# A transformer stack with its residual stream kept centred: layer norms that skip the mean, and variances and their spread in column and row groups

## The reference

```python
def _layernorm(x, axis=-1, eps=1e-05):
    m = jnp.mean(x, axis=axis, keepdims=True)
    v = jnp.var(x, axis=axis, keepdims=True)
    return (x - m) / jnp.sqrt(v + eps)

x = x + windowed_attention(_layernorm(x))      # stage 0, 16 heads of 8, output weights Wo
x = x + ffn(_layernorm(x))                     # stage 1, ternary weights, bias
x = x + gated_recurrence(_layernorm(x))        # stage 2, ends in gelu(..) @ ld_W + ld_b + identity
x = x + ffn(_layernorm(x))                     # stage 3, the same weights as stage 1
x = x + full_attention(_layernorm(x)) + bo     # stage 4, Wo of layer 1
x = x + moe(_layernorm(x))                     # stage 5, top-1 router over 8 experts, one shared We
x = x + full_attention(_layernorm(x))          # stage 6, W_out
x = x + moe(_layernorm(x))                     # stage 7, the same weights as stage 5
```

## Time and profile before

| | us |
|---|---|
| median of three runs | 1211.13 |
| the profiled execution, device time | 1204.97 |
| its span in the profile | 1203.2 |
| PE busy | 1051.9 (87%) |
| DVE busy | 864.4 (72%) |
| ACT busy | 748.8 (62%) |
| POOL busy | 90.4 (8%) |

### The profile page before, as it was taken

The page is one execution under the profiler, slowest core; times in us unless marked ns, Lnnn a source line. Parts: engine busy times, 40 slices in busy tenths (PEclk is TensorE's granted clock), DMA queues, the critical chain, the costliest instruction groups (busy, mean ns, idle before and its releaser), DMA issues.

```text
span 1203.2 us, 31909 instructions
## 1 busy us (share of the span) xinstructions
PE 1051.9 (87%) x13025; PEld 484.6 (40%) x13025; DVE 864.4 (72%) x1151; ACT 748.8 (62%) x1510; POOL 90.4 (8%) x370
## 2 busy tenths in 40 slices
PE   7598999794587999899999998779898899999986
PEld 3344545442253333334444344442333334344443
DVE  3553654345554799899999944555999999999635
ACT  2422545237213389889999982231888899999921
POOL 8000100000000000000000000000000000000000
PEclk9897999888778999999999997789999999999978
DMA  3473432100006322220101000044313201001000
GB/s 96 138 211 72 98 92 74 39 1 1 0 0 189 86 64 63 55 51 18 29 19 24 24 20 10 1 124 140 71 44 72 53 18 25 22 18 30 18 15 35
DMA packets 73825, 64.97 MB, mean 54 GB/s; under 512 B 27792, under 2 KB 53648, under 8 KB 73552
## 3 DMA queue, kind: packets, MB, share of 16 engines
q1 hardware_dynamic: 73680, 62.94, 20.0%
HBM read 27.06 MB, written 35.85 MB: 52 GB/s over the span
## 4 chain that ended last, share of the span: by engine, by line
DVE 43%; PE 38%; DMA 7%; issue 4%; ACT 4%; SPq 3%; DVEq 0%; ACTq 0%
DVE nmf L1331 35%; PE wide L556 24%; PE bank L556 14%; DMA KQs<-m_dram 4%; ACT xcsq L949 2%; DVE xcsq L1148 1%; DVE res L1148 1%; SPq L378 1%; DVE nmt L1290 1%; ACT big L949 1%; SPq L309 1%; DVE big L1410 1%; SPq L299 1%; DVE x L1148 1%; DMA qf_dram<-big 1%
## 5 line engine op out<-in xcount | busy, mean ns | idle before, releaser
L1331 DVE TENSOR_REDUCE nmf<-wide 128x1 f32<-128x1024 f32 x512 | 587.3, 1204 | 40.4 <-PE wide L556 40.3
L949 ACT ACTIVATE big<-wide 128x512 f32<-128x512 f32 (+1 forms) x703 | 403.4, 601 | 81.1 <-PE wide L556 54.7
L556 PE MATMUL wide<-big,KQs 48*128 48x512 bf16 (+1 forms) x1376 | 349.4, 344 | 4.3 <-DVE nmf L1331 3.3
L556 PE MATMUL bank<-big,V 128*9 128x128 f32 x8192 | 319.9, 274 | 12.5
L556 PE MATMUL wide<-KQs,big 50*128 50x512 bf16 (+1 forms) x1035 | 266.9, 324 | 11.9 <-DMA KQs<-m_dram 10.8
L556 PEld LDWEIGHTS bank<-big,V 128*9 128x9 f32 x8192 | 176.8, 90 | 233.7 <-ACT big L949 221.7
L949 ACT ACTIVATE big<-bank 128x512 f32<-128x512 f32 (+2 forms) x473 | 233.8, 516 | 23.2 <-PE bank L556 10.6
L556 PE MATMUL bank<-KQs,big 50*128 50x512 bf16 x341 | 130.3, 382 | 6.8 <-DMA KQs<-m_dram 6.8
L556 PEld LDWEIGHTS wide<-KQs,big 50*128 50x128 bf16 x1035 | 70.6, 95 | 117.9 <-ACT big L949 56.5
L1296 DVE TENSOR_REDUCE nmw<-wide 95x4 f32<-95x512 f32 (+1 forms) x96 | 61.2, 640 | 58.9 <-PE wide L556 57.9
L949 ACT ACTIVATE xcsq<-xcsq 128x512 f32<-128x512 f32 x32 | 20.1, 630 | 124.2 <-DVE xcsq L1148 124.2
(11 more groups left out here) (175 smaller groups left out, 833.3 us busy)
## 6 DMA issues: line engine op xcount, KB each, us to landing
o_dram<-big SPq DMA_DIRECT2D x128, 64.0 KB
big<-kf_dram SPq DMA_DIRECT2D x32, 200.0 KB
kf_dram<-big SPq DMA_DIRECT2D x24, 256.0 KB, 4.2
qf_dram<-big SPq DMA_DIRECT2D x24, 256.0 KB, 4.0
KQs<-qf_dram SPq DMA_DIRECT2D x32, 192.0 KB
ow_dram<-scr SPq DMA_DIRECT2D x32, 142.5 KB
big<-kw_dram SPq DMA_DIRECT2D x16, 275.0 KB
kw_dram<-scr SPq DMA_DIRECT2D x12, 352.0 KB, 5.7
```

Source lines behind the costliest of these rows:

```text
L556: return nc.tensor.matmul(o, l, r, start=start, stop=stop, **kw)
L949: return nc.scalar.activation(o, i, f, **kw)
L1331: nc.vector.tensor_reduce(nmf[:, (s0 + i) % 4, c:c + 1], wide[:, k:k + 2, :].rearrange("p g c -> p (g c)"), AX.X, ALU.max, negate=True).th ...
```

## The change

1. **Weights and biases centred.** After the ternary matrix is built in stage 0, DVE takes from each of five output weight matrices (`wo0`, `ld`, `wo1`, `wo2`, the ternary one) its mean over output channels, kept in `wmean`, and from three bias columns their channel mean, summed in `bmean`. So stages 0 to 4 and 6 add nothing to the channel mean of `x`.
2. **Means in a side tile.** `track` multiplies `wmean`'s column, broadcast to 32 columns, with the input of each output projection: four matmuls of 128 columns, each into its own group of 32 partitions of bank 0. ACT copies that bank in the next norm (`keep_means`), and POOL adds it to `mrow` (`add_means`).
3. **Layer norm.** Means are computed only in stages 0 and 6 (`MEANS`), where `x` is centred in place. In the others ACT squares `x` itself. The variance of a chunk comes from four matmuls with 32 columns of `meanw` as weights, each into its group of 32 partitions; root and reciprocal work on 128 x 128; and the spread is four matmuls over 32 partitions each, with a selector `rowsel` as weights, into four banks (0 to 3). The diagonal is gone. `normalise` reads the four banks.
4. **Work called inside the norm.** In stages 1, 3, 5 and 7 the first `ffn` or `logits` step of a chunk stands between PE's third and fourth spread, the other three behind the fourth.
5. **Mixture of experts.** Two of the `we` matmuls move behind `tri` and `ones`; ACT evacuates the `we` products with their bias instead of the gates. In stage 7 the tracked mean and `bmean` are added back to `x` by `true_x`, four DVE operations in two pairs, after 16 matmuls that spread `mrow`.
6. `keep_busy` in stage 0 also waits for `b_sum`, and POOL's first constants are joined by `rowsel` (five memsets).

```diff
@@ constants, POOL
             step(pool.memset(meanw[:, :], 1.0 / P))
+            step(pool.memset(rowsel[:, :], 0.0))
+            for g in range(4):
+                step(pool.memset(rowsel[32 * g:32 * g + 1, :], 1.0))
...
+            def add_means(t):
+                pool.wait_ge(mt_evac, t + 1)
+                pool.tensor_tensor(mrow[:, :], mrow[:, :], mtmp[:, :], ALU.add).then_inc(mt_add, 1)
@@ PE
+            def track(c, i, chunk):
+                for g in range(4):
+                    ins = mm(bk(TRACK)[32 * g:32 * g + 32, P * c:P * c + P], wmean[:, i:i + 1].broadcast_to((P, 32)),
+                             chunk[:, P * g:P * g + P])
+                if c == NC - 1:
+                    ins.then_inc(mt_mm, 1)
...
                 def variance(c):
                     pe.wait_ge(ln_sq, NC * k + c + 1)
-                    if c:
-                        pe.wait_ge(ln_std, NC * k + c)
-                    for t in range(4 * c, 4 * c + 4):
-                        ins = mm(bk(3)[:, t:t + 1], sq[:, P * t:P * t + P], meanw[:, 0:1])
+                    if c >= 2:
+                        pe.wait_ge(ln_std, NC * k + c - 1)
+                    for g in range(4):
+                        ins = mm(bk(4 + c % 2)[32 * g:32 * g + 32, 0:P], meanw[:, 0:32], xch(sq, c)[:, P * g:P * g + P])
                     ins.then_inc(ln_var, 1)
 
                 def spread(c):
-                    pe.wait_ge(ln_diag, NC * k + c + 1)
-                    if c == 2:
-                        pe.wait_ge(xn_ready, NC * k + 1)
-                    mm(bk(LN_STD[c]), ones[:, :], res[:, c % 2, :]).then_inc(ln_b, 1)
+                    pe.wait_ge(ln_rstd, NC * k + c + 1)
+                    if c == 0:
+                        pe.wait_ge(mt_evac, tracked + 1)
+                    else:
+                        pe.wait_ge(xn_ready, NC * k + c)
+                    for g in range(4):
+                        ins = mm(bk(g)[:, P * c:P * c + P], rowsel[32 * g:32 * g + 32, :],
+                                 ln_rstd_s[32 * g:32 * g + 32, P * c:P * c + P])
+                    ins.then_inc(ln_b, 1)
...
-                for step, c in ((mean, 0), (mean, 1), (variance, 0), (mean, 2), (variance, 1), (spread, 0),
-                                (mean, 3), (variance, 2), (spread, 1), (variance, 3), (spread, 2), (spread, 3)):
-                    step(c)
+                if k in MEANS:
+                    for step, c in ((mean, 0), (mean, 1), (variance, 0), (mean, 2), (variance, 1), (mean, 3)):
+                        step(c)
+                else:
+                    variance(0)
+                    variance(1)
+                spread(0)
+                variance(2)
+                spread(1)
+                variance(3)
+                spread(2)
+                if after:
+                    after(0)
+                spread(3)
+                if after:
+                    for c in range(1, NC):
+                        after(c)
...
+                mm(bk(6)[:, 8:11], meanw[:, :], bias[:, BI["ld_b"]:BI["ld_b"] + 3]).then_inc(b_mean, 1)
                 mm(bk(6)[:, 0:1], ones[:, :], ts_[:, 0:1]).then_inc(tw_sum, 1)
...
                 pe.wait_ge(tw, 2)
+                pe.wait_ge(b_sum, 1)
                 keep_busy(2, bk(6))
...
                     pe.wait_ge(at_out, NC * layer + c + 1)
+                    track(c, 1 + layer, xch(aT, c))
                     mm(bk(4 + c), w("wo%d" % layer), xch(aT, c)).then_inc(o_mm, 1)
...
+                mm(bk(4 + c), tern[:, :], xn(c)).then_inc(f_mm, 1)
+                if c == NC - 1:
+                    for j in range(NC):
+                        track(j, 4, xn(j))
+            def logits(k, c):
+                pe.wait_ge(xn_ready, NC * (5 + 2 * k) + c + 1)
+                for t in range(4 * c, 4 * c + 4):
+                    ins = mm(bk(4)[:, t * E:(t + 1) * E], xnt(t), wgs[:, :])
...
             def moe(k):
...
+                if k:
+                    pe.wait_ge(mt_add, 7)
+                    for c in range(NC):
+                        for g in range(4):
+                            ins = mm(bk(g)[:, P * c:P * c + P], rowsel[32 * g:32 * g + 32, :],
+                                     mrow[32 * g:32 * g + 32, P * c:P * c + P])
+                    ins.then_inc(mt_spread, 1)
+                expert(0)
+                expert(1)
                 pe.wait_ge(moe_const, 1)
                 pe.wait_ge(m_dve, M_DVE * k + 10)
-                mm(bk(1)[:, 0:P], tri[:, :], moh[:, :]).then_inc(m_pe, 1)
-                mm(bk(2)[:, 0:P], ones[:, :], moh[:, :]).then_inc(m_pe, 1)
+                mm(bk(6)[:, 0:P], tri[:, :], moh[:, :]).then_inc(m_pe, 1)
+                mm(bk(6)[:, P:2 * P], ones[:, :], moh[:, :]).then_inc(m_pe, 1)
+                if k:
+                    pe.wait_ge(x_out, NC)
+                expert(2)
+                expert(3)
@@ ACT
+                def keep_means():
+                    act.wait_ge(mt_mm, tracked + 1)
+                    if tracked >= 2:
+                        act.wait_ge(mt_add, tracked - 1)
+                    fn(mtmp[:, :] if tracked else mrow[:, :], bk(TRACK), ACT.Copy).then_inc(mt_evac, 1)
+
+                square(0)
+                square(1)
...
+                else:
+                    keep_means()
+                    root(0)
+                    square(2)
+                    root(1)
+                    square(3)
+                root(2)
+                root(3)
@@ DVE
                 def rstd(c):
                     dve.wait_ge(ln_std, NC * k + c + 1)
-                    r = ln_s[:, 1, 4 * c:4 * c + 4]
-                    nc.vector.reciprocal(r, ln_s[:, 0, 4 * c:4 * c + 4]).then_inc(ln_rstd, 1)
...
-                    spread(c % 2, r).then_inc(ln_diag, 1)
+                    nc.vector.reciprocal(ln_rstd_s[:, P * c:P * c + P], ln_std_s[:, P * c:P * c + P]).then_inc(ln_rstd, 1)
 
                 def normalise(c):
                     dve.wait_ge(ln_b, NC * k + c + 1)
-                    tt(xn(c), xch(xc, c), bk(LN_STD[c]), ALU.mult).then_inc(xn_ready, 1)
...
+                    tt(quarters(xn(c)), quarters(xch(x, c)), wide[:, 0:4, P * c:P * c + P], ALU.mult).then_inc(xn_ready, 1)
+
+                if k in MEANS:
+                    for c in range(NC):
+                        centre(c)
+                for step, c in ((rstd, 0), (rstd, 1), (normalise, 0), (rstd, 2), (normalise, 1), (rstd, 3),
+                                (normalise, 2), (normalise, 3)):
                     step(c)
...
+                def true_x(c):
+                    if c == 0:
+                        dve.wait_ge(mt_spread, 1)
+                        dve.wait_ge(b_sum, 1)
+                    v = quarters(xch(x, c))
+                    nc.vector.scalar_tensor_tensor(v, wide[:, 0:4, P * c:P * c + P], bmean[:, 0:1], v, ALU.add,
+                                                   ALU.add).then_inc(x_out, 1)
...
                     ternary()
+                    centre_biases()
+                    centre_weights()
                     zero_heads()
```

More of the change, by code:

```diff
@@ L543, in _ @@
                     split_shift(u, nmw[0:QT, u % 4, :], QT)
+            for t in range(1, min(nst, 4)):
+                add_means(t)
             for layer in (1, 2):
                 if nst > 2 * layer + 2:
+                    add_means(2 * layer + 2)
                     for i in range(SLOTS):
@@ L934, in _ @@
                 if stage in (1, 3):
-                    ffn(stage // 2)
+                    layernorm(stage, stage, lambda c: ffn(stage // 2, c))
                 if stage == 2:
@@ L1125, in moe @@
                 for c in range(NC):
-                    act.wait_ge(m_pe, M_PE * k + 7 + c + 1)
-                    fn(xch(mgb, c), bk(c), ACT.Copy).then_inc(m_act, 1)
+                    act.wait_ge(m_pe, M_PE * k + (2 + c if c < 2 else 4 + c))
+                    fn(xch(mgb, c), bk(WE[c]), ACT.Identity, bias=bcol("be")).then_inc(m_act, 1)
             act.wait_ge(ln_const, 1)
             for stage in range(nst):
-                layernorm(stage)
+                layernorm(stage, stage)
                 if stage == 0:
@@ L1173, in layernorm @@
-                for step, c in ((centre, 0), (centre, 1), (centre, 2), (rstd, 0), (centre, 3), (rstd, 1),
-                                (normalise, 0), (rstd, 2), (normalise, 1), (rstd, 3), (normalise, 2), (normalise, 3)):
-                    step(c)
+                    tt(quarters(xn(c)), quarters(xch(x, c)), wide[:, 0:4, P * c:P * c + P], ALU.mult).then_inc(xn_ready, 1)
+                if k in MEANS:
+                    for c in range(NC):
+                        centre(c)
+                for step, c in ((rstd, 0), (rstd, 1), (normalise, 0), (rstd, 2), (normalise, 1), (rstd, 3),
+                                (normalise, 2), (normalise, 3)):
+                    step(c)
@@ L1177, in ternary, with centre_biases @@
+            def centre_biases():
+                dve.wait_ge(b_mean, 1)
+                m = bk(6)[:, 8:11]
```

(8 more changed lines are left out.)

124 lines of the change are left out of this document (84 added, 40 removed).

## The result

The changed kernel took 1177.65 us in the median of four runs (1174.44 to 1179.17); the kernel before took 1213.99 us beside it (four runs, 1206.11 to 1218.67). The ratio is 0.970, with a 95% interval of 0.964 to 0.976: faster by 36 us, where 39 were forecast. The profiled execution after is the slowest of its four (1179.17 us, span 1177.2 us); the one before (1204.97 us, span 1203.2 us) is faster than all four beside the change. So the two traces differ by only 26.0 us, and what follows accounts for these 26.

What follows compares the result with a forecast made beforehand. Attentions hold most of the chain but stay; the gain lies in norms, chains of hand-overs between engines. Terms -41 - 8 + 0.8 + 4.5 - 5.9 + 8.3 + 2 = -39.3 us give 1172 us, range 1153 to 1192.

Steps and rivals of the forecast that it cites:

- The norms: Six norms without means: 49.9 us against 90.8, so -41 us, bounds -46 and -36.
- R: In six norms without means, end of the first root counted from the last addition to `x`: 4.65 us in sum.
- Rival 1: Float32 row pieces of spreads do not overlap: 1186 us at full clock (chance 0.13), about 1212 at half (0.05).
- Rival 3: Changes of tiling drain PE, about 60 on the path: at 0.85 us more each 1223 us, slower; chance 0.04.
- the first matmuls at 1.2 GHz: Behind norms, two to four matmuls opening recurrence and both projections cost 0.86 us more each: +4.5 us (0, +8).
- Rival 2: PE stays at 1.2 GHz in all short stages, everything at its upper bound: -20 us, 1191 us; chance 0.06.
- Tracks: Tracks ahead of output projections in stages 0, 4 and 6, three times four, mostly at 1.2 GHz: +8.3 us (+5, +9).
- `b_sum`: In stage 0 the `keep_busy` block starts later, waiting for the bias operations: +2 us (+1.7, +2.3), all on the chain.
- `centre_weights`: In stage 0 it delays `zero_heads` by 3.4 us, within the `keep_busy` block's 4.91 us: nothing.
- GpSimd's additions: POOL's additions of the means fall after its attention loops or ahead of them with microseconds to spare: nothing.
- Stage 0 behind its norm: The rest of stage 0 after its norm, holding shares of the terms given as sums over stages: +4.9 us.
- The mixture of experts: Stages 5 and 7: logits -2.3 us each, shorter router chain in stage 5, `true_x` +0.6; sum -5.9 us (-9, -2).

Runs made afterwards that it cites:

- full-row spreads: Changed kernel with each spread as four matmuls over all 128 rows, one after another, in place of four row pieces: 1174.14 us, ratio 0.975.
- filled norms: Changed kernel with filling matmuls that nobody waits for in every norm but the first: 1153.98 us, ratio 0.956.
- last group: Last three experiments, sharing runs of the kernel before (1205 us); among them the changed kernel again, unedited: 1173.79 us, ratio 0.973.

## Why the prediction was right, and where its sum was not

**The norms.** The sum for six norms was 49.9 us and they took 50.11; the step by step working holds in kind: DVE busy in 6 of 8 us, pieces in 0.50 us. Two of its terms were off and cancel: R, between -0.2 us (stage 3) and 1.14 us, sums to 3.2 us for 4.65, and what follows R, with the inserted work, to 46.9 us for 45.2. Stage 0 gained 5.5 us and stage 6 3.9, for 4 and 4.

**Rival 1** (row pieces one after another) falls by the trace. The full-row spreads also show that its price in the norms was about right, 17.2 us for 14, and its total was not: as much came back behind the norms, with a better clock there, and the time did not move.

**Rival 3** (changes of tiling drain). A track with its two changes goes at a pace of 0.58 us at 1.2 GHz and 0.36 us at 2.4, for 0.43 and 0.21 us of columns, so a block with its changes costs some 0.15 us beyond its columns; 0.65 us more each would have been needed. The rule of the Trainium skill, TensorEngine Tiling (Array Packing), section Key Properties, that a change of tiling mode drains TensorE, may hold, but here the drain is no dearer than this.

**The step that was mis-sized** is "the first matmuls at 1.2 GHz", +4.5 us. It was the right mechanism: the prediction says that a norm now leaves TensorE nearly idle, which overstates it (4.0 to 6.8 us of 8.4 busy) but points the right way. But it priced two to four matmuls behind three norms. The filled norms show 16 to 20 us in the traces behind stage 0, and 18 to 24 us between the medians. What the step left out: the second part of each full projection and the block behind it (stage 4's first maximum comes 30.7 us after its norm, and came 27.2 us after it before the change: 3.5 us, where the step gave a projection some 1.5), the logits (2.3 us forecast as a gain, 0.2 measured in stage 5, since the 24 instructions that were left ran at 0.21 us each; with the filled norms the first reduction comes 3.27 us after the norm there and 2.40 us in stage 7, for 4.74 and 4.71 before the change), the mixtures of experts to their end (2.6 us in stage 7), and `ffn`.

**Rival 2** (1.2 GHz in all short stages), given 0.06, is the one that came nearest to what was missed: TensorE was at 0.58 to 0.83 of full speed in the norms and at 0.69 behind that of stage 1. The time stayed inside the range since the norms' gain was so large.

**Tracks** +8.3: a pace of 0.58 us each in stages 4 and 6, where 0.72 was priced (at most 2.3 us of a stage; the loops and the start hold the rest of the +6.1 and +7.8), 0.36 in stage 0, where 1.2 GHz had been assumed. **`b_sum`** +2: 1.5. **`centre_weights`** at nothing: the trace shows no wait for it. **GpSimd's additions** at nothing: one collided with DVE for 1 us, and cost about 0.1. **Stage 0 behind its norm** came out at +7.4 for 4.9: the block of filling matmuls was 2.8 us longer in this execution (7.73 against 4.91), for which a part of the wait is neither shown nor ruled out, and the tracks were cheaper.

**The mixture of experts** -5.9, measured -1.7: the router's chain of stage 5 gave its 2.0 us and the logits next to nothing in either stage, which is nearly all of the 4.2 us that are missing. Stage 7 as a whole came out 0.7 us longer, where the chain with `true_x` was allowed 0.6.

**Against the median** 36.3 us were gained for 39.3 forecast, and in the profiled executions 26.0; the difference is that the one before was faster than all four runs beside the change and the one after the slowest of its four. The changed kernel beside the last group gained 30.8 us (1204.62 to 1173.79). Part of the closeness is therefore luck: the term of the clock was too small by far, in a sum whose largest term was right.

## What to carry to other kernels

Before work is taken off TensorE between two stretches that need it, look at the granted clock of these stretches: matmuls that nobody waits for may be holding it up, and the bill comes in the next stage, not where the work was removed. Seven to eleven filling matmuls per norm were worth 16 to 24 us here and nothing in the kernel whose norms were still full. And when a change has two halves, time one alone: the groups, with the means kept, brought nothing in the total.

## What the runs showed of the hardware

Doubling a spread's work cost no time in the total. Full-row spreads made the norms 17.2 us longer and the rest 22.2 us shorter, and the mean clock went from 0.900 to 0.926.

DVE's addition with both operands in SBUF stands still while GpSimd adds: it started 0.14 us after GpSimd's and ended 0.55 us after it, in 1.67 us; in the second execution of the same kernel it started 0.66 us after GpSimd's, took 1.15 us and again ended 0.55 us after it. DVE's additions from PSUM and its reciprocals of one SBUF operand kept their 0.69 and 0.9 us beside the same instruction on GpSimd (247.66, 1.76 us for two). This is what the Trainium skill, SBUF — State Buffer, section Who interferes with whom, states: a DVE instruction with two SBUF inputs contends with a GpSimd instruction that reads SBUF, one with at most one such input does not (outside the 2-port modes). The trace agrees.

Logits, 128 columns of weights for 8 columns of data, take 0.11 us for each instruction at 2.4 GHz and 0.21 us at 1.2 GHz (24 in 2.69 and in 5.12 us). A row of them did not hold the clock: in stage 5 it fell to half within the row before the change, and again with the filled norms, where 24 that began at full clock took 3.98 us and the matmul behind them ran at 1.2 GHz (2.06 us for two instructions of 512 columns). In the trace with full-row spreads it did not fall.
